# A two-layer graph network on one core: order of the head, waits of the scatters, first ring turn and last steps of layer 2

## What is computed

```python
x = layernorm(x + L0(x, (src, dst), edge_attr_32, node_vec1, ...))
x = layernorm(x + L1(x, node_vec1, edge_attr_16, edge_attr_4, src, dst, ...))

# L0: messages from the features of dst, summed over src
tp  = fctp_messages(node_features[dst], edge_attr, W1, W2, W3, W4)
agg = segment_sum(tp @ Wm + bm, src, N_NODES)
out = node_features + concat([node_features, agg]) @ Wu + bu

# L1: messages from the features of src, averaged over dst
w   = silu(edge_scalars @ Wfc1) @ Wfc2
mid = products of w, f[src] and edge_attr_sh
n   = segment_sum(mid, dst, N) / clip(count, 1)
out = sc + alpha * (n @ Wl2)
```

## Time and profile before

| | us |
|---|---|
| median of 3 runs | 5759.57 (5759.46 to 5767.8) |
| the profiled execution | 5760.69 |
| its span | 5758.9 |

### The profile page before, as it was taken

One profiled execution on the slowest core, in us unless ns is written; L12 is line 12 of the kernel. 1 busy time (PEld: TensorE's weight loads), 2 busy tenths in 40 slices (PEclk: granted clock), 3 DMA queues, 4 the chain that ended last, 5 costly groups with the idle time before them and its releaser, 6 DMA issues. The chain is left out here.

```text
span 5758.9 us, 109402 instructions
## 1 busy us (share of the span) xinstructions
PE 4257.5 (74%) x31805; PEld 3204.8 (56%) x31805; DVE 3701.5 (64%) x7179; ACT 1385.8 (24%) x3804; POOL 3186.2 (55%) x3214
## 2 busy tenths in 40 slices
PE   4777777777777777769997676777767767776766
PEld 3555555555555555559996454545444445545444
DVE  8776667677767665558884555555555555555555
ACT  3433333333333333310003111111111111111111
POOL 1666666666666666650003566656665565555654
PEclk9877777887777777779998777777777777777777
DMA  7444444444444444449992222222222222222222
GB/s 167 110 110 113 110 112 113 113 110 109 112 112 112 113 111 111 113 145 303 302 289 78 58 59 59 59 59 60 59 59 59 59 58 59 59 57 58 60 59 42
DMA packets 605069, 591.90 MB, mean 103 GB/s; under 512 B 183845, under 2 KB 486662, under 8 KB 604662
## 3 DMA queue, kind: packets, MB, share of 16 engines
q1 hardware_dynamic: 420070, 256.17, 18.6%
q0 software_dynamic: 151488, 262.69, 17.0%
q10 hardware_dynamic: 33424, 72.03, 3.8%
HBM read 431.87 MB, written 158.72 MB: 103 GB/s over the span
## 5 line engine op out<-in xcount | busy, mean ns | idle before, releaser
L2995 POOL DMA_INDIRECT q_fg<-f,q_index x1568 | 1552.0, 990 | 1039.8 <-issue 484.1
L1141 POOL DMA_INDIRECT messages<-stage,place x1568 | 1572.7, 1003 | 884.4 <-issue 507.4
L1445 PE MATMUL ps_m<-by_attr,turned 128*128 128x160 f32 x6272 | 1163.1, 340 | 239.2 <-issue 231.4
L1445 PEld LDWEIGHTS ps_m<-by_attr,turned 128*128 128x128 f32 x6272 | 1057.9, 217 | 387.2 <-issue 378.2
L3249 PE MATMUL q_ps_m<-q_prod,q_onehot_sh 128*32 128x160 f32 x12544 | 824.2, 375 | 361.7 <-issue 217.8
L3057 DVE SCALAR_TENSOR_TENSOR q_sums<-q_ps_m,split_q,q_sums 128x161 f32 x784 | 301.6, 385 | 1041.0 <-issue 935.9
L1223 DVE SCALAR_TENSOR_TENSOR turned<-rel_row,quarter,flipped 128x512 f32<-128x512 uint8 x784 | 528.2, 746 | 637.8 <-remote 542.8
L3249 PEld LDWEIGHTS q_ps_m<-q_prod,q_onehot_sh 128*32 128x32 f32 x12544 | 485.3, 133 | 621.2 <-issue 391.3
L3236 PE MATMUL q_ps_w<-q_wfc,q_hidden 64*128 64x192 f32 x3136 | 615.4, 435 | 253.6 <-issue 237.3
L3236 PEld LDWEIGHTS q_ps_w<-q_wfc,q_hidden 64*128 64x128 f32 x3136 | 381.8, 237 | 397.7 <-issue 354.0
L1366 ACT COPY stage<-ps_m 128x320 f32<-128x320 f32 x784 | 317.0, 437 | 1112.8 <-remote 818.0
(11 more groups left out here) (282 smaller groups left out, 4248.9 us busy)
## 6 DMA issues: line engine op xcount, KB each, us to landing
nat<-in_edge_attr SPq DMA_DIRECT2D x392, 256.0 KB
rows_in<-messages ACTq DMA_DIRECT2D x208, 324.0 KB, 3.4
rows_in<-messages SPq DMA_DIRECT2D x208, 324.0 KB, 3.4
rel_row<-rel_rows SPq DMA_DIRECT2D x98, 256.0 KB
messages<-stage,place POOLq DMA_INDIRECT x1568
q_fg<-f,q_index POOLq DMA_INDIRECT x1568
q_a<-in_edge_attr SPq DMA_DIRECT2D x196, 64.0 KB
messages<-zeros SPq DMA_DIRECT2D x31, 324.0 KB, 8.0
```

The costliest lines, as they stand in the source:

```text
L1141: nc.gpsimd.indirect_dma_start(out=msgs, out_offset=bass.IndirectOffsetOnAxis(ap=place[:, r, k:k + 1], axis=0), in_=stage[:, r, k, :], in_ ...
L1445: last = nc.tensor.matmul(ps_m[g % BANKS][:, k % 2 * D0:k % 2 * D0 + D0], turned[:, r, half, k * P:(k + 1) * P], by_attr[:, r, k, :, half] ...
L2995: nc.gpsimd.indirect_dma_start(out=fg[:, i, place_of(v), :], out_offset=None, in_=f_tab, in_offset=bass.IndirectOffsetOnAxis(ap=index[:, i ...
```

## The change

In the head, POOL now clears `stage` first, then makes the five tables once `first_i` has landed, then waits for `s_ends` and clears `by_node`, and then writes 16 fills instead of 12 (ACT 2 instead of 6, SP 31 as before). `neg_f` overwrites `first_f` instead of a piece of `dst_t`. ACT's finds are put between the node copies. In layer 1 both gates on `s_msg` are gone. In layer 2 the gathers of the first ring turn don't wait for steps; the slots of the last three adds are read in the last iteration; the finish of tile ROUNDS-3 stands behind these adds on DVE, and its deviation behind both takes on ACT.

```diff
-                neg_f = dst_t[0:1, :, :].rearrange("o b e -> o (b e)").bitcast(fp32)[:, 0:TILES].rearrange("o (n k) -> o n k", k=EP)
+                neg_f = first_f
-                FILLS_ACT = range(3, SRC_BUCKETS, 8)
-                FILLS_POOL = range(1, SRC_BUCKETS, 4)
+                FILLS_ACT = (3, 27)
+                FILLS_POOL = range(1, SRC_BUCKETS, 3)
...
                         nc.gpsimd.memset(zeros[:, :], 0.0).then_inc(s_made, 16)
+                        nc.gpsimd.memset(stage[:, :, :, :], 1.0)
+
+                        pool.wait_ge(s_first, 16)
+                        nc.gpsimd.tensor_scalar(first_f[:, :, :].rearrange("o n k -> o (n k)"), first_i[:, :], float(N_NODES - 1), None, ALU.min).then_inc(s_base, 1)
...
+                        pool.wait_ge(s_ends, 1)
                         for r in range(2):
                             nc.gpsimd.memset(by_node[:, r, :, :], 0.0).then_inc(s_blank_y, 1)
-                        nc.gpsimd.memset(stage[:, :, :, :], 1.0)
-                        pool.wait_ge(s_ends, 1)
...
-                                if first and r == 0:
-                                    pass
-                                elif g == 0:
-                                    pool.wait_ge(s_msg, n * PAIRS0 + 2 * PAIRS0)
-                                elif g == HALF0 and not last:
-                                    pool.wait_ge(s_msg, n * PAIRS0 + 2 * PAIRS0 + HALF0)
                                 pool.wait_ge(s_mev, n * PAIRS0 + (BANKS + g + 1))
...
-                        if not isinstance(n, int) or n >= 3:
+                        if not isinstance(n, int):
                             stepped(pool, n - 3)
...
-                            if h == 3 and tile is not None:
+                            if h == 3 and tile is not None and not last:
                                 finish(tile)
...
+                            if last and h == AHEAD - 1:
+                                late_slots.extend(slots_of(2 * BATCHES - LATE + n) for n in range(LATE))
...
                         stepped(dve, j)
-                        add(j - LATE, 1 - j % 2)
+                        add(j - LATE, 1 - j % 2, late_slots[j - 2 * BATCHES])
+                    finish(ROUNDS - 3)
                     normalise(ROUNDS - 3)
...
-                    deviation(ROUNDS - 3)
                     take(ROUNDS - 2, 4 * BATCHES)
                     take(ROUNDS - 1, 4 * BATCHES, last_full)
+                    deviation(ROUNDS - 3)
```

More of the change, by code:

```diff
@@ L1123, in _, with scatter @@
                     def _(pool):
-                        def scatter(t, r, first=False, last=False):
+                        def scatter(t, r, first=False):
                             n = t * 2 + r
@@ L3047, in message, with slots_of, add @@
                         last.then_inc(s_msg, 1)
-                    def add(j, g):
-                        slots = [dve.value_load(slot_q[0:1, c, bass.ds(j, 1)], min_val=0, max_val=SLOTS_E) for c in range(2)]
+                    def slots_of(j):
+                        return [dve.value_load(slot_q[0:1, c, bass.ds(j, 1)], min_val=0, max_val=SLOTS_E) for c in range(2)]
+                    def add(j, g, slots=None):
+                        slots = slots or slots_of(j)
                         dve.sem_inc(s_begun, 1)
```

44 lines of the change are left out of this document (25 added, 19 removed).

## The result

The changed kernel takes **5796.5 us** (median of 6 runs, 5780.37 to 5803.18); the kernel before, measured again beside it, 5759.51. The ratio is 1.0066, 95% interval [1.0045, 1.0087]: 37 us slower, where I forecast 39 us faster. The profiled execution took 5802.27 us, its span is 5800.3, 41.4 us over that of before.

The account below looks back on a forecast made before the run. POOL was taken to bound layer 1, plus a stop per epoch, and DVE the head; 14 + 19 + 3 + 3 = 39 us off 5760.69 gave 5721.7, set at 5720 for the median, range 5640 to 5800.

Parts of the forecast that it names:

- Layer 1: Layer 1's scatters: removing POOL's two waits gives 7.4 + 11 and rounding, 19 us less; one pause per sixteen scatters remains.
- The first 7.4 us: Layer 1's second epoch: of POOL's 7.68 us stop ahead of 171.81, all but the usual 0.30 goes.
- The 11 us for runs of eight: Layer 1, mid-epoch stops: 19 epochs split into runs of eight each save 0.57 us without the wait, 11 us.
- eights everywhere: Rival in layer 1: POOL starts on the first pair and pauses twice per epoch; 5777 to 5804, say 5790; chance 0.26.
- The 0.23 us per epoch: Layer 1: extra epoch time from which the eights rival decides, the other 22 us of gain over 98 epochs.
- Head: Before layer 1, four edits: 4.3 + 3.5 + 9.1 - 3 = 14 us less, with ends at 17 and 5.
- Tables on POOL: Head: 3.5 us leave DVE's path; POOL takes 3.2 to 12.2 us, of which 3 us come back through DVE.
- a rival at 9 us: Head: POOL's tables hold DVE by the skill's lock, 9 us of the head come back, 5729; chance 0.07.
- ACT's order: Head: finds placed where ACT waited for PE, so all 9.06 us of DVE's wait for find(5) go.
- the cover I named for the head's end: Head: SP's fills, 46.77 us, move ahead with s_ends to about 98, before DVE's end near 101.
- Start of layer 2: Layer 2's first ring turn: gathers without the wait run ahead, 3 us less; ends 11 less and 7 more.
- End: Final serial chain: finish behind late adds and slots preloaded, 4.6 us less before slot loads, 3 taken; ends 5.5 and 0.

Follow-up runs that it names:

- the first alone: Changed kernel with only the wait on s_msg at an epoch's first pair put back: ratio 1.0375, 216 us over before.
- before without waits: Kernel before with only POOL's two scatter waits on s_msg removed: ratio 1.0068, 40 us over before.

## Why the prediction was wrong, point by point

**Layer 1: wrong in sign.** I took 19 us less and it was 50.7 us more in the profiled run. The step that failed is "in the long run what counts is how much the producers finish per pause": that a pause comes once per sixteen scatters whatever POOL waits for. The runs show that a stop's number and length both depend on the waits: 1.32 x 2.96 us with both, 1.49 x 3.13 with none, 1.14 x 5.65 with the first alone. I also took it that the producers stand still only because signals are held; PE itself issues its products late while POOL streams, for 1.9 us per epoch before and 3.1 after by the idle stretches counted above. The 18.6 us in which the producers "make an epoch while nothing holds them" are a rate of the first five epochs alone: of any five in a row after the first six, none took under 21.9 us each in that trace. The first 7.4 us came at their place (the stop of 7.68 is gone; instead there are 3.20 ahead of 168.14 and 1.57 ahead of 171.94): the second epoch starts 27.6 us after the first scatter instead of 35.5. By the fourth epoch 5.1 us of it are left, and the later stops take more than all of it. The 11 us for runs of eight had the wrong sign: the wait in mid-epoch, whose stops I had priced as pure loss, keeps the stop at the epoch's start short. Taking away only that wait costs 231 us (6057.3 against 5826.7 on one chip).

The rival "eights everywhere" gave 5790 and the measured time is 5796.5. Its size was right and so was its kind, POOL starting on too little and pausing more often. But plain eights aren't what the trace shows. That would be two stops per epoch; it has 1.49, after runs of very different length, and each of them is a little longer than before. That its number came within 7 us is in part luck. The 0.23 us per epoch from which it was to decide came from 22 us of other gains; these add up to 20 us, or 27 with the 7.4, so it should have been 0.20 or 0.28.

**Head: right in sign, 14 us expected, 6.4 found.** Late clearing: as worked out (L855 at 7.19 with 1.03 us; counting from 15.7). Tables on POOL: 10.5 us of POOL's time, within my 3.2 to 12.2; what came back through DVE is the end of the counting, at 48.7 instead of 15.7 + 25.9 = 41.6: 7.1 us where I took 3. With the tables on DVE the counting takes 26.3 us again. The trace agrees with the Trainium skill's rule on the shared pair (SBUF — State Buffer, section Who interferes with whom), which I had priced as a rival at 9 us: three `in_t` took 5.60 us instead of 1.6 beside a table of 4.60. ACT's order: DVE's wait went, but the cover I named for the head's end failed: SP's fills took 52.18 us and not the old 46.77, and they began 2.1 us later instead of moving ahead, so that they ended at 110.1 and not 98. They don't hang on `s_ends` alone: SP first issues two loads of `rel_row`, which need `rel` from DVE, and `rel` stands behind the comparisons that the tables held (47.91 instead of 45.37). With the loads go the fills, 56.28 and 57.93 instead of 54.16 and 55.81. The queues look like one stream: SP's 31 and POOL's 16 fills of 324 KB in 52.2 us are some 300 GB/s, 31 and 12 in 46.8 us before the same rate. If so, fills moved from ACT's tail to POOL lengthen the stretch; no run has the new head with the old sharing of the fills.

**Start of layer 2: wrong on these chips.** 3 less expected; 3.7 to 6.6 more found at the 129th gather (3.6 in the two profiles of the result), and nothing that can be measured over the whole layer: the 3.1 us less from first to last gather are within what such kernels differ by (2587.9 to 2594.5 on one chip). My bad end was one more stop like that of 6.67 us. What came is one stop of 18.3 in place of 11.0 and 3.5, and a first message 20 us later. On the other kind of chip the open ring wins some 8 us.

**End: right as a mechanism.** The last regular add and the last take, first in before (its take is at 5734.09), then in the changed kernel:

```profile
5722.22 0.39 DVE L3057 SCALAR_TENSOR_TENSOR q_sums<-q_ps_m,split_q,q_sums 128x161 f32 x1 [1.82 <-PE q_ps_m L3252]
```

```profile
5769.01 0.91 DVE L3065 SCALAR_TENSOR_TENSOR q_sums<-q_ps_m,split_q,q_sums 128x161 f32 x2
...
5776.33 0.73 ACT L3169 COPY q_full<-q_sums 128x644 f32 x1 [10.69 <-DVE q_sums L3065]
```

The take stands 7.32 us behind the add instead of 11.87, 4.5 us of the 4.6 worked out. In the two profiles little of it reaches the sum (0.6 us less from the last gather to the end), since the stretch from the last gather to the last regular add grew from 12.66 to 17.57 us; it is 10.2 to 17.6 in the other kernels on the slower chips too, whatever the end. On the chip of 5842 us the whole stretch is 46.2 us with the old end (before without waits) and 39.4 to 42.0 in the three kernels with the new one. What the slot loads cost, which I took as 1.6 us, no row shows by itself.

**Chances and range.** The range held the time, by 3.5 us; the forecast and its sign were wrong, and 0.24 for slower was too little. A count over all epochs, which I hadn't made, could have warned: of the 93 epochs of before 86 have a stop at their start, of 3.17 us, and 24 one in the middle, of 2.75 us. The waits made the stops regular in place and length, and I priced them from a few rows.

## What to carry to other kernels

A wait that looks like pure loss in the rows where it is seen can still be what keeps two engines in step. Before it is taken away, price what happens when it is missed, not only what it costs. And of two rate-limiting engines that disturb each other, the number and length of stops is the quantity to count, over all epochs, before any single stop is read as a loss.

Where a head ends with a stream of transfers, time saved on an engine beside the stream counts only as far as the stream's end: of 9.9 us of waiting that the order of ACT took away, 5.6 to 8.2 came through. And look what the stream itself waits for before its start is moved in a sum.

## What the runs showed of the hardware

The kernel before differs by 19 to 20% between chips: 5760 to 5842 us on the slower ones, 4848 to 4851 on two others, at the same duration of a scatter (0.96 us in the median of every profile). Of the 978 us between the changed kernel's two profiles 375 are in layer 1's scatters (2445.7 against 2070.3) and 583 in layer 2's gathers (2584.4 against 2001.4); the other 20 are 7.7 between the layers, 13.4 after the last gather and 1.5 the other way in the head. What differs is PE while POOL streams. On the slower chips PE stands idle without a releaser: counted over 0.4 us, 540 us between the first and the last scatter of before and 428 of the changed kernel, and 466 and 468 us in layer 2 (from the 33rd gather to the last). On the faster chips the same count gives nothing for the changed kernel, in either layer. With it go ACT's copies into `stage`: waits of 9.46 us in the earlier trace rows, ended 2.2 us after POOL went quiet, and at most 1.71 us for PE on the faster chips. The mean granted clock of PE is lower too, 0.78 against 0.83 in layer 1 of the changed kernel's two profiles (from 200 to 2500 and to 2100 us), both a mix of the two levels; in the node stage it is 0.99 in both, the upper level. Whether the clock is a cause or follows from the gaps, and what holds PE, was not found. A change that acts on it has opposite signs on the two: the changed kernel is 0.66% slower on one kind and 0.62% faster on the other.

A POOL instruction on one partition can hold DVE's comparisons for nearly its whole time: three that take 1.6 us alone took 5.60 us beside 4.60 us of POOL.
